# Selective scan on one core: the gate product taken from VectorE and split into a ScalarE copy and a GpSimd product

## The reference, cut to what matters

```python
xz = x @ W_in                                  # 256 -> 1024
x_inner, z = jnp.split(xz, 2, axis=-1)         # 512 each
xc = silu(conv4(x_inner) + conv_b)             # depthwise, causal
x_ssm = xc @ W_xproj                           # 33 rows: delta, B (16), C (16)
delta = softplus(delta_raw * w_dt + b_dt)
h_t = exp(delta * A) * h_(t-1) + delta * B * xc    # 16 states for each of 512 channels
y = sum_n(h * C) + xc * D_param
y = y * jax.nn.silu(z)                         # the gate
return y @ W_out
```

## Time and profile before

| | busy us | share of the span |
|---|---|---|
| TensorE (PE) | 2628.8 | 86% |
| VectorE (DVE) | 2162.7 | 71% |
| GpSimd (POOL) | 1729.4 | 57% |
| ScalarE (ACT) | 1469.8 | 48% |
| span of the profiled execution | 3044.5 | |
| time of the profiled execution | 3046.24 | |
| median of the timed runs | 3042.44 | |

### The profile page before, as it was taken

One profiled execution on the slowest core, in us unless ns is written; L12 is line 12 of the kernel. 1 busy time (PEld: TensorE's weight loads), 2 busy tenths in 40 slices (PEclk: granted clock), 3 DMA queues, 4 the chain that ended last, 5 costly groups with the idle time before them and its releaser, 6 DMA issues. The chain is left out here.

```text
span 3044.5 us, 32684 instructions
## 1 busy us (share of the span) xinstructions
PE 2628.8 (86%) x7774; PEld 1299.6 (43%) x7775; DVE 2162.7 (71%) x2367; ACT 1469.8 (48%) x2717; POOL 1729.4 (57%) x864
## 2 busy tenths in 40 slices
PE   4689898888979889897888978887569999999999
PEld 2234343343434334343333434333236666666665
DVE  0599999989999998998999999999632222222222
ACT  2565656656555665665666565665212222222222
POOL 1566767777685767768676676777422222222222
PEclk9899899999999999999999999999879999999999
DMA  1321303223040321303123140321432222222222
GB/s 38 126 101 37 144 27 134 78 75 131 21 145 27 132 92 60 140 16 141 56 103 117 36 144 26 132 86 64 165 80 44 43 45 44 44 44 44 45 44 31
DMA packets 125600, 235.91 MB, mean 77 GB/s; under 512 B 46449, under 2 KB 93714, under 8 KB 109122
## 3 DMA queue, kind: packets, MB, share of 16 engines
q1 hardware_dynamic: 98342, 200.56, 19.2%
q0 software_dynamic: 26128, 34.36, 6.5%
q10 hardware_dynamic: 1036, 0.09, 0.0%
HBM read 182.22 MB, written 53.78 MB: 78 GB/s over the span
## 5 line engine op out<-in xcount | busy, mean ns | idle before, releaser
L536 POOL TENSOR_TENSOR arena<-u,arena 128x2048 f32<-128x2048 f32 x256 | 1157.9, 4528 | 357.2 <-DVE psum L927 355.9
L1244 PE MATMUL psum<-hc,ident 128*128 128x512 f32 x2048 | 1060.8, 645 | 272.6 <-DVE hc L935 272.4
L927 DVE TENSOR_TENSOR_SCAN psum<-psum,arena 128x1024 f32<-128x1024 f32 x512 | 1172.9, 2291 | 124.4 <-ACT psum L732 83.2
L1244 PEld LDWEIGHTS psum<-hc,ident 128*128 128x128 f32 x2048 | 379.7, 200 | 836.6 <-DVE hc L935 485.5
L732 ACT ACTIVATE psum<-delta,a_neg 128x508 f32<-128x508 f32 x1024 | 656.4, 674 | 0.6
L935 DVE TENSOR_TENSOR hc<-psum,arena 128x1024 f32<-128x1024 f32 x512 | 626.0, 1223 | 19.9 <-DVE psum L927 4.8
L615 POOL DMA_INDIRECT out_dram<-hres,tok_id x136 | 211.1, 1552 | 599.4 <-ACT hres L864 550.0
L1375 PE MATMUL psum<-arena,xnt 128*128 x1088 | 516.0, 597 | 0.0
L1129 DVE COPY z<-psum 128x512 f32<-128x512 f32 x136 | 94.1, 692 | 458.0 <-PE psum L1384 458.0
L864 ACT ACTIVATE hres<-psum,tok_w 128x256 f32<-128x256 f32 x136 | 64.3, 473 | 454.4 <-PE psum L1394 447.7
L1394 PE MATMUL psum<-arena,z 128*128 x1088 | 257.1, 379 | 0.9 <-DVE z L1129 0.9
(11 more groups left out here) (145 smaller groups left out, 1921.4 us busy)
## 6 DMA issues: line engine op xcount, KB each, us to landing
arena<-ssm_rows SPq DMA_DIRECT2D x128, 1024.0 KB, 5.9
delta<-expert_rows SPq DMA_DIRECT2D x136, 129.0 KB, 2.0
h_saved_rows<-hnew SPq DMA_DIRECT2D x16, 512.0 KB, 6.5
hres<-h_saved_rows SPq DMA_DIRECT2D x16, 512.0 KB
out_dram<-h SPq DMA_DIRECT2D x16, 512.0 KB, 3.0
draw<-ssm_rows SPq DMA_DIRECT2D x16, 256.0 KB, 3.2
arena<-in_L_ffn_wg_dram SPq DMA_DIRECT2D x8, 512.0 KB
arena<-in_L_ffn_wi_dram SPq DMA_DIRECT2D x8, 512.0 KB
```

Source lines behind the costliest of these rows:

```text
L536: pool.tensor_tensor(dBx[k % 2], rep, b_rep[:, q * QN:(q + 1) * QN, :], ALU.mult).then_inc(dbx_ready, 1)
L927: nc.vector.tensor_tensor_scan(h, h, src, 0.0, ALU.mult, ALU.add).then_inc(scan_done, 1)
L1244: last = nc.tensor.matmul(yacc[(k // HC) % 2], ident[:, :], hc[k % 2][:, i, :], start=False, stop=(k % HC == HC - 1 and i == 1))
```

## The change

The gate of a finished bank is no longer one VectorE product that reads PSUM. ScalarE copies the finished bank into yz (`evac_y`, in its steps 9, 17, 25 and, for the last quarter, step 1 of the next group), and GpSimd multiplies yz by z in place (`gate_y`, behind its dBx 7, 11, 15 and, for the last quarter, dBx 2 of the next group). GpSimd can't use the bank, so a new semaphore `y_copied` stands between the two; TensorE's skip now waits for the copy, not for the product. The wait of `evac_z` for `gate_done` is as before and now means GpSimd's product. The second rsqrt of a group moves on GpSimd from behind dBx 5 to behind dBx 6. In the tail, GpSimd's product comes first, ahead of `second_row`.

```diff
@@ gpsimd
+            def gate_y(g, c):
+                if c == 0:
+                    pool.wait_ge(z_ready, g + 1)
+                pool.wait_ge(y_copied, NCH * g + c + 1)
+                pool.tensor_tensor(yz[:, c, :], yz[:, c, :], z[:, c, :], ALU.mult).then_inc(gate_done, 1)
...
                         add_delta(g, c)
                         make_u(g, par, c)
+                    if k == 2 and not first:
+                        gate_y(g - 1, NCH - 1)
+                    if k in (7, 11, 15):
+                        gate_y(g, (k - 7) // NCH)
                     if not second:
                         if k == 0:
                             second_row(g - 2)
...
-                        if k == 5:
+                        if k == 6:
                             rsqrt(g - 1, 1, stat2, pow2)
...
             def tail(g):
+                gate_y(g, NCH - 1)
                 second_row(g - 1)
@@ scalar
+            def evac_y(g, c):
+
+                actq.wait_ge(sum_done, HU * g + HC * (c + 1))
+                if c == 0:
+                    ahead(actq, o_full, 2 * g)
+                nc.scalar.activation(yz[:, c, :], yacc[c % 2], ACT.Copy).then_inc(y_copied, 1)
...
+                    if k == 1 and not first:
+                        evac_y(g - 1, NCH - 1)
+                    if k in (9, 17, 25):
+                        evac_y(g, k // HC - 1)
                     if k < NCH:
                         evac_z(g, k)
...
             def tail(g):
+                evac_y(g, NCH - 1)
                 norm2(g, 0)
@@ vector
-            def gate_y(g, c):
-                dve.wait_ge(sum_done, HU * g + HC * (c + 1))
-                if c == 0:
-                    dve.wait_ge(z_ready, g + 1)
-                    ahead(dve, o_full, 2 * g)
-                nc.vector.tensor_tensor(yz[:, c, :], yacc[c % 2], z[:, c, :], ALU.mult).then_inc(gate_done, 1)
...
                     scan(g, k)
-                    if k == 1 and not first:
-                        gate_y(g - 1, NCH - 1)
-                    if k in (11, 19, 27):
-                        gate_y(g, (k - 11) // HC)
                     times_c(g, k)
...
             def tail(g):
-                gate_y(g, NCH - 1)
                 residual(g, 0)
@@ tensor
             def skip(g, par, c):
-                ahead(pe, gate_done, NCH * g + c - 1)
+                ahead(pe, y_copied, NCH * g + c - 1)
```

More of the change, by code:

```diff
@@ L238, in audio_tower @@
         sum_done = sem("sum_done")
+        y_copied = sem("y_copied")
         gate_done = sem("gate_done")
```

## The result

The changed kernel takes 3060.07 us (median of 5, 3053.69 to 3061.62), the kernel before 3042.44 us on the same chip (median of 5, 3041.62 to 3043.66). The ratio is 1.0054, with a 95% interval of 1.0039 to 1.0069: slower, by 17.6 us in the medians. The profiled execution of the changed kernel has a span of 3059.9 us against 3044.5: 15.4 us.

The account below looks back on a forecast made before the run. VectorE was taken to set the pace, busy 121.6 of 131 us a group. Terms +14.0 + 12.8 - 2.7 - 1.1 + 1.2 = +24.2 us gave 3066.6 us against the timed median 3042.44; range 3044 to 3077.

Parts of the forecast that it names:

- case (a): Rival: only z bank 3 is late and TensorE's clock stays up; 3053.9 us, chance 0.23 for 3045 to 3058.
- The sign: Whole kernel: slower by over 0.2% (6.1 us), above 3048.5 us, chance 0.78.
- The saving on VectorE: Between scan and C product: each of 64 removed gates costs 0.46 us, so at most 29.4 us gained.
- The late z bank: Start of O groups: GpSimd's last-quarter product delays z bank 3 and scan 5 by 1.75 us, 14.0 us in all.
- O groups: Groups 2, 3, 5, 7, 9, 11, 13, 14, not starting at the loop's back edge; expected to lose 1.75 us each.
- E groups: Groups 4, 6, 8, 10, 12, starting at the loop's back edge; no loss expected from the late z bank.
- The clock: Scan 5 to 10: O groups fall to half clock like E groups, 8 x 1.6 = 12.8 us added.
- The gates in the middle: Gates 11, 19, 27: 0.21 us gained in 13 groups (2.7 us); 1.1 us estimated for groups 0 and 1.
- The tail: Behind the last sums: copy 0.60 and product 1.27 us replace VectorE's 0.67 us gate, +1.2 us.
- Covers: Existing waits hide added ScalarE copies and GpSimd work; uncovered, copies would cost 2.2 us a group.
- cover of dBx 3: Before scan 6: dBx 3, 1.27 us later, hidden by 0.5 us in O groups; otherwise up to 1.3 us a group.

Follow-up runs that it names:

- One part alone: Kernel before with only the last quarter's gate moved to ScalarE and GpSimd, the other three left on VectorE: 3072.68 us, ratio 1.0090.
- the second bank: Changed kernel plus separate banks for quarter 3 of z in even and odd groups: 3052.46 us, ratio 1.0022 to the kernel before.
- changed kernel with filler: Changed kernel plus two more 128x512 TensorE matmuls, results not used, during the wait for the residual in step 6: 3025.66 us, ratio 0.9938.
- kernel before with filler: Kernel before plus two more 128x512 TensorE matmuls, results not used, during the wait for the residual in step 6: 3031.5 us, ratio 0.9957.
- both gaps filled: Unused matmuls added at the residual and in step 23, GpSimd reordered: 3011.15 us with the change and a second bank for z's quarter 3, 3015.32 without.

## Why the prediction was right or wrong

**The range and the sign.** 3060.07 lies in 3044 to 3077, between the forecast (3066.6) and case (a) (3053.9), and 0.2 us nearer to case (a); the five executions reach from 3053.69 to 3061.62. The sign was forecast, and for the causes that the runs show. That the time fell into the narrower 3058 to 3074 is partly luck: gates and clock came out 10.3 us below the forecast, and waits that it put at nothing gave 2.8 us of them back.

**The saving on VectorE, 0.46 a gate.** Right where it could be seen: 0.45 in each of 15 groups from scan 10 to 21. My mark of 43 us less busy time was wrong; 31.4 were measured, since neighbours overlap in the busy count too.

**The late z bank, +14.0.** Right in mechanism and size: +13.0 between scans 29 and 5, of it 13.45 in the 8 O groups (1.63 to 1.71 each), -0.4 in E. One part alone reproduced it (13.4 in the O groups), the second bank removed it (0.15). z bank 3 came at the 27.41 us that I had named and on the product that I had named; scan 5's idle time is 1.59 us, a little under the 1.8 that I had set as a mark.

**The clock, +12.8.** Right in mechanism, mis-sized in this profile. 5 of the 8 O groups (3, 5, 9, 11, 14) are 1.62 us longer between scans 5 and 10; in 2, 7 and 13 the clock held. Group 1 lost the fall it had (-1.68). So the clock gave 8.1 - 1.7 = 6.4 us, half of what I put. With the last quarter alone all 8 fell. I had assumed one outcome for all groups. The gap was the same 2.08 us in those where it fell and in those where it held; the other parts of the change shift each group by tenths of a microsecond, and that this decides it is argued, not shown.

The stretch as a whole is longer by 9.2 us, and the other 2.8 are not the clock's. Group 15 pays 1.3 and the E groups and group 2 pay 0.2 to 0.3 each, and they pay the same in the changed kernel with filler, at full clock. In group 15 it is the late dBx 3, here with the filler:

```profile
2064.09 2.30 DVE L951 TENSOR_TENSOR_SCAN psum<-psum,arena 128x1024 f32<-128x1024 f32 x1 [1.20 <-POOL arena L543]
```

In the E groups scan 9 waits longer for ScalarE (1.87 us in group 8 of the changed kernel with filler, 1.59 in the kernel before with filler); the cause stays open.

**The gates in the middle, -2.7 and -1.1.** The step that failed: the term was put at half of what it gave. Gate 11 came back whole, -7.7 in all (two gates in group 15), where I gave it 0.21 us a group and group 15 nothing. I took TensorE's idle time before the sums of step 11 as all it could gain. The starts tell it better. TensorE before, the sums of steps 10 and 11 in group 8; then the same of the changed kernel:

```profile
1194.34 1.98 PE L1244 MATMUL psum<-hc,ident 128*128 128x512 f32 x4 [0.51 <-DVE hc L935]
...
1198.26 1.98 PE L1244 MATMUL psum<-hc,ident 128*128 128x512 f32 x4 [0.21 <-DVE hc L935]
```

```profile
1198.58 1.98 PE L1256 MATMUL psum<-hc,ident 128*128 128x512 f32 x4 [0.67 <-DVE hc L959]
...
1202.12 1.91 PE L1256 MATMUL psum<-hc,ident 128*128 128x512 f32 x4
```

From start to start 3.92 us became 3.54: 0.38 of the 0.45. So the idle time in brackets (0.21 us) understates what a start can gain. That gates 19 and 27 give nothing was right: in the changed kernel scans 21 and 29 wait 0.89 and 0.84 us for ScalarE in group 8, where they waited 0.46 and 0.39.

**The tail, +1.2.** The rest column has 2.1. TensorE now waits 2.03 us for the product instead of 0.78, +1.25. The projection behind it then takes 5.41 us instead of 3.72: the clock is granted at 0.68 in this stretch. Behind the same 2.03 us it held in the changed kernel with filler (3.72 us). The rest, up to the first expert tile and behind it, is 0.8 shorter.

**Covers.** The copies of the first three quarters and the products behind dBx 7, 11 and 15 show no cost: with these alone none of the three stretches from scan 5 to 29 is longer in sum. The cover of dBx 3 held only where scan 5 was late: it failed in group 15 of the changed kernel, and with the second z bank the price showed in all O groups, 1.20 us at scan 6.

**The sum.** 13.0 + 9.2 - 7.7 - 1.2 + 2.1 = 15.4 us in the profiled execution, against 24.2 forecast. Between the two are 8.8 us: the clock accounts for 6.4 from scan 5 to 10, the gates for 3.9, the late z bank for 1.0, and 1.2 come from scan 21 to 29, where the half clock behind step 23 fell on other groups; against these stand the 2.8 us of waits that I had not counted and 0.9 of the tail.

## What to carry to other kernels

When an operation moves to another engine, look first at who waits for its result there: here an operation of 1.3 us behind a long one cost 13 us, where the whole relief of the busy engine brought 7.7. A saving on the bounding engine ends at the next wait of that engine, so count it stretch by stretch between waits; and read waits from start to start. Before taking work off a busy engine, look whether TensorE stands waiting in short gaps each round: keeping it busy in one of them brought 14 us by itself, where moving gates brought 4 to 6 us against the same kernel without the move.

## What the runs showed of the hardware that I had not expected

Two matmuls a group that nobody needs (1.88 us) took 34 us off the changed kernel, some 3 of them by the wait in group 15; the granted clock, mean of the span, rose from 0.957 to 0.969. The length of the gap before the residual doesn't settle alone whether the clock falls behind it. In the O groups it held in all 8 behind 1.73 us (kernel before) and behind the 0.36 us that the filler leaves in the changed kernel. Behind 2.08 us it held in 3 of 8 in the changed kernel and in none with the last quarter alone, and behind 2.95 us, with the second z bank, in 2 of 8. Kernels with such gaps scatter between executions (3030.56 to 3045.96 us with the first three gates moved), those with both gaps filled less (3010.76 to 3011.62, and 3014.47 to 3016.32 without the change). Why the filler at the residual also removed the half clock behind step 23 in the changed kernel, and in the kernel before only in part, was not tested: the gap there is the same (2.50 and 2.49 us), so the gap alone does not decide; that it is a shift by tenths of a microsecond is argued, not shown.
